# Attention step: where the turned rows and the turned context stand on TensorE, and the context copy on ScalarE

## What is computed

```python
x = x + tanh(g_xattn[0]) * attention(layernorm(x), ctx, ctx, mask, Wq, bq, Wk, bk, Wv, bv, Wo, bo)
# attention, for each sequence:
q = heads(query @ Wq + bq) / 4
k = heads(key @ Wk + bk)
v = heads(value @ Wv + bv)
scores = where(mask == 0, -1e20, q @ k.T)
out = (softmax(scores) @ v) @ Wo + bo
```

## Time and profile before

| | us |
|---|---|
| median of 3 runs | 705.67 |
| lowest, highest | 705.29, 708.04 |
| span of the profiled execution | 705.0 |
| TensorE busy in it | 640.0 (91%) |
| VectorE, ScalarE, GpSimd busy in it | 423.2, 303.0, 266.6 |

### The profile page before, as it was taken

How to read it: one execution, slowest core, us unless ns; L and a number is a source line. 1 busy time by engine, 2 the same in 40 slices (tenths; PEclk the granted TensorE clock), 3 DMA queues, 4 the chain that set the end, 5 groups by cost and what they waited for, 6 DMA issues and landing times.

```text
span 705.0 us, 14478 instructions
## 1 busy us (share of the span) xinstructions
PE 640.0 (91%) x5191; PEld 465.1 (66%) x5191; DVE 423.2 (60%) x1287; ACT 303.0 (43%) x632; POOL 266.6 (38%) x388
## 2 busy tenths in 40 slices
PE   7899999999999988869999999999899999992990
PEld 5465655777777755557656665657788888882880
DVE  6654756898999658863112222112668988883671
ACT  2323235787878825343221222220555555510750
POOL 4101202454554521043465445233211334355475
PEclk9999999999999999989999999999999999996996
DMA  8659853778775229881563894323613494123652
GB/s 276 204 155 212 220 105 87 126 130 125 125 127 92 94 75 160 269 264 32 101 146 39 243 291 96 71 30 46 223 61 121 151 308 164 61 91 102 205 163 80
DMA packets 101278, 99.95 MB, mean 142 GB/s; under 512 B 22182, under 2 KB 91305, under 8 KB 101204
## 3 DMA queue, kind: packets, MB, share of 16 engines
q1 hardware_dynamic: 91992, 82.57, 46.1%
q0 software_dynamic: 9216, 16.46, 10.3%
HBM read 61.20 MB, written 38.05 MB: 141 GB/s over the span
## 4 chain that ended last, share of the span: by engine, by line
PE 49%; DVE 6%; issue 2%; DMA 2%; POOL 2%; ACT 1%; POOLq 0%; SPq 0%; DVEq 0%; ACTq 0%
PE pc L1705 10%; PE pc L1682 9%; PE pc L2541 4%; PE pc L2274 4%; PE pc L2269 3%; PE pc L1065 3%; PE pc L2310 2%; PE pc L2267 2%; PE pc L1658 2%; PE pc L2251 2%; PE pc L1701 2%; POOL result L2446 1%; PE pc L2332 1%; PE pc L1670 1%; PE pc L1685 1%
## 5 line engine op out<-in xcount | busy, mean ns | idle before, releaser
L1522 POOL DMA_INDIRECT scratch_resid<-y,k_idx x32 | 54.8, 1714 | 81.8 <-DVE y L1590 80.9
L506 DVE TENSOR_REDUCE neg_max<-pb_two 128x8 f32<-128x1024 f32 x64 | 78.1, 1220 | 12.2 <-PE pb_two L836 9.2
L671 ACT ACTIVATE probs<-pb_two,b_key_cols 128x1024 f32<-128x1024 f32 x64 | 76.9, 1202 | 16.0 <-PE pb_two L860 16.0
L1705 PE MATMUL pc<-w_dn,mid 128*128 128x256 f32 x320 | 73.3, 384 | 0.0
L1633 ACT ACTIVATE mid<-pc,b_up 128x512 f32<-128x512 f32 x35 | 24.1, 687 | 109.7 <-PE pc L1682 109.7
L1705 PEld LDWEIGHTS pc<-w_dn,mid 128*128 128x128 f32 x320 | 59.5, 190 | 12.7 <-issue 5.3
L1682 PE MATMUL pc<-gT,w_up 128*128 128x512 f32 x140 | 61.2, 592 | 0.0
L1590 DVE TENSOR_SCALAR y<-pc,gate 128x256 f32<-128x256 f32 x32 | 15.4, 484 | 64.6 <-PE pc L1705 46.8
L1513 POOL DMA_INDIRECT rows<-scratch_rows,k_idx x32 | 32.0, 999 | 53.6 <-DVE k_idx L1366 37.9
L1682 PEld LDWEIGHTS pc<-gT,w_up 128*128 128x128 f32 x140 | 26.6, 190 | 30.5 <-issue 30.1
L1572 DVE COPY gT<-pc 128x512 f32<-128x512 f32 x7 | 4.8, 692 | 61.0 <-PE pc L1670 61.0
(11 more groups left out here) (381 smaller groups left out, 1417.5 us busy)
## 6 DMA issues: line engine op xcount, KB each, us to landing
qs<-scratch_qparts SPq DMA_DIRECT2D x48, 128.0 KB, 4.2
ks<-scratch_kparts SPq DMA_DIRECT2D x48, 128.0 KB
w_dn<-in_W_down SPq DMA_DIRECT2D x8, 640.0 KB
scratch_slots<-s_zero SPq DMA_DIRECT2D x1, 4160.0 KB, 18.8
cT<-in_ctxT SPq DMA_DIRECT2D x8, 512.0 KB, 6.5
s_x<-in_x SPq DMA_DIRECT2D x8, 512.0 KB, 6.9
scratch_rows<-s_x SPq DMA_DIRECT2D x16, 256.0 KB, 4.2
scratch_resid<-s_x SPq DMA_DIRECT2D x8, 512.0 KB, 7.1
```

The source lines that it names most:

```text
L506: V.tensor_reduce(neg_max[:].rearrange("p (b u j) -> p u b j", b=2, u=2)[:, u], ps_both[0][:].rearrange("p (b j k) -> p b j k", b=2, j=4), ...
L671: A.activation(probs[t % 2 * 2 + u][:], ps_both[1][:].rearrange("p (h q) -> p h q", h=HEADS // 2), ACT.Exp, bias=key_cols[:, 1, t:t + 1], ...
L1522: pool.indirect_dma_start(out=T["resid"], out_offset=bass.IndirectOffsetOnAxis(ap=S["idx"][:, e, c:c + 1], axis=0), in_=y[e % 2][:, c, :], ...
L1705: ins = nc.tensor.matmul(here(c), mid[e % 2][m][:, c * P:(c + 1) * P], w_dn[e % 2][:, m, :], start=False, stop=(m == MT - 2))
```

## The change

On TensorE `turn_rows` and `turn_context` leave the end of step s and stand in step s+1 behind `scores(s+4,0)`, ahead of `max_T`. On ScalarE `rows_out` comes one step later and directly behind the first exponentials, and `context_out` comes behind the second exponentials. `rows_out(t)` gets one more wait, for `max_T(t+5)`, and `max_T(t)` now waits for one copy of rows fewer, since both share bank 6. No instruction that computes is added or removed.

```diff
             def rows_out(t):
                 act.wait_ge(aT_ps, t + 1)
+                act.wait_ge(nmT_ps, min(t + 6, TILES))
...
             for s in range(1, END):
                 if is_tile(s):
                     exponentials(s, 0)
+                if is_tile(s - 3):
+                    rows_out(s - 3)
                 if is_tile(s + 2):
                     max_out(s + 2)
+                if is_tile(s):
+                    exponentials(s, 1)
                 if is_tile(s - 1):
                     context_out(s - 1)
-                if is_tile(s):
-                    exponentials(s, 1)
-                if is_tile(s - 2):
-                    rows_out(s - 2)
...
             def max_T(t):
                 pe.wait_ge(nm_s, t + 1)
-                if t >= 5:
-                    pe.wait_ge(aT_s, t - 4)
+                if t >= 6:
+                    pe.wait_ge(aT_s, t - 5)
...
                 if is_tile(s + AHEAD):
                     scores(s + AHEAD, 0)
+                if is_tile(s - 3):
+                    turn_rows(s - 3)
+                if is_tile(s - 2):
+                    turn_context(s - 2)
                 if is_tile(s + 2):
                     max_T(s + 2)
...
-                if is_tile(s - 2):
-                    turn_rows(s - 2)
-                if is_tile(s - 1):
-                    turn_context(s - 1)
```

## The result

| | before | changed |
|---|---|---|
| median of 11 runs each, us | 706.23 | 710.91 |
| ratio of changed to before, 95% interval | | 1.0052 (1.0032 to 1.0073) |
| second comparison (6 and 10 runs): median, us | 706.07 | 713.51 |
| ratio, 95% interval | | 1.0094 (1.0059 to 1.0129) |
| span of the profiled execution, us | 705.0 | 709.4 |

The change is slower, by 0.5% in the first comparison and 0.9% in the second; the intervals overlap between 0.6 and 0.7%. The medians lie 4.7 us (0.66%) and 7.4 us (1.05%) apart. A time lies 1.7 to 2.3 us over the span of its own execution (711.17 and 709.4 for the profiled one of the changed kernel). The 0.7 us between span and median before was therefore not what lies around the span: it set two different executions side by side, and by these differences the profiled one took about 707 us (an estimate), more than the median of 705.67.

What follows compares the result with a forecast made beforehand. TensorE, nearly without breaks, was taken to bound the loop, VectorE close behind. Steady steps +3.8 and filling +0.4 gave +4.2 us on a span of 705.0: 709.2, median 709.9; own range 708 to 711.5, overall range 702.5 to 713.

Steps and rivals of the forecast that it cites:

- rival C: Moved maxima come late, so six waits grow: 2.4 us more, up to 4 with a larger `output` break, 712 to 714; chance 0.14.
- filling: Pipeline start: `turn_context(0)` leaves a wait in step 1 for step 2, +0.4 us, between bounds of 0 and 1.0.
- 25 steps: Steady attention loop: each step 0.15 us longer, +3.8 us in all, some 109 us long instead of 105.2.
- draining: Last steps, without scores: longer first half traded for shorter second, same work, end of chain unchanged, 0.
- The wait for ScalarE: TensorE ahead of `shifted(s,1)`: real wait 0.11 us of 0.31 idle, in 24 steps, 2.6 us to win at most.
- The first half: TensorE's first half of a steady step, with the six turns moved in: 2.46 us after, against 1.70.
- The second half: TensorE's second half of a steady step: about 1.71 us against 2.32, closed by ScalarE (1.70) and VectorE (1.73) loops.
- The step: One steady step of the attention loop: 4.17 us against 4.02, so +0.15.
- the reason given for it: Steady step: three changes from float32 to bf16 instead of two, and two new loops, traded for one 0.11 us wait.
- The moved maxima: Maxima in SBUF 0.4 us later, about 2.2 behind the step's start; longer steps give 0.45 back, net 0.
- A: TensorE's breaks are waits, VectorE becomes the bound: 4.0 us faster, 701.7, down to 698; chance 0.14.
- B: The trade comes out even: step 4.02 to 4.08 us, 0 to +1.5, so 705 to 707.5; chance 0.27.

Runs made afterwards that it cites:

- add_bf16_full: Kernel before plus one bf16 transpose with 128x128 weights between `output` and the turned rows; second half of the step 2.38 us against 2.32.
- add_f32: Kernel before plus one float32 transpose with 128x128 weights between `output` and the turned rows; second half of the step 2.43 us against 2.32.
- context_only: Kernel before with only `turn_context` moved, behind `max_T` and ahead of the contexts, ScalarE order kept; 714.89 us against 706.88, ratio 1.0096.
- add_bf16: Kernel before plus one bf16 turn with 128x32 weights between `output` and the turned rows; second half of the step 2.63 us against 2.32.
- add_short: Kernel before plus one float32 transpose with 49x128 weights between `output` and the turned rows; second half of the step 2.66 us against 2.32.
- copy_late_alone: Kernel before with only `context_out` put behind the second exponentials, TensorE's order kept; one time of 718.2 us.
- copy_early: Changed kernel with `context_out` put back ahead of the second exponentials; 715.38 us, ratio to the kernel before 1.0112.
- drain_copy: Changed kernel with `context_out` of tile 30 put ahead of the last exponentials, in step 31 alone; one time of 709.62 us.

## Why the prediction was right, and where it was not

*The size.* Forecast +4.2 us or 0.6% and a median of 708 to 711.5. The first comparison gave 710.91, inside; the second 713.51, outside, among the numbers of rival C. The sum is right in part by luck, as its terms show (means of two traces of the changed kernel less means of three of the kernel before):

| | forecast | traces |
|---|---|---|
| up to `shifted(0,0)` | 0 | +1.6, with the same code |
| filling, to `shifted(4,0)` | +0.4 | +1.3 (-0.5 and +3.0) |
| 25 steps | +3.8 | +1.0 |
| draining, to the last `output` | 0 | +1.5 |
| all that follows | 0 | -0.4 |
| span | +4.2 | +4.9 |

The 25 steps should have taken some 109 us and took 107.8 and 106.4. The term of the steps was too large by what the stalls gave back, and terms put at nothing or little made up for it. With so few traces the terms are known to 1 us at best, the draining excepted.

*The wait for ScalarE.* Read as 0.11 and not 0.31 per step. Confirmed: with the cover in place the loads still idle for 0.20 ahead of `shifted(s,1)`. Who had taken the 7.9 us of the waits view as the prize would have expected three times too much.

*The first half.* Forecast 2.46, measured 2.42. The six turns took 0.81 from start to `max_T` (0.80 forecast). The term that was off is `max_T`: 0.08 was carried over from a place where it had been waited for; in the stream it is 0.01.

*The second half.* Forecast 1.71, measured 1.76. The break behind `output` was 0.09 where TensorE came late (0.10 forecast, 0.27 feared; the sum for the lower bound, 1.92 - 1.84, is 0.08 and not 0.09). The loop with ScalarE is what binds, but the step from the end of the exponentials to `shifted` is 0.11 there and not 0.06.

*The step.* +0.15 forecast, +0.165 measured. It is made up of 0.06 by which the turns take longer in their new place (0.81 for 0.75), 0.09 for the break behind `output`, and 0.12 to 0.13 for the new wait in the second half, less the old wait of 0.11 in the first. The two waits all but cancel; the breaks are what was lost.

*What failed is the reason given for it.* "The step had two changes from float32 to bf16 and has three" is true as a count and false as a cause. The runs showed that a change of type with full weights costs nothing, and that a change of the weights' rows or columns does. The prices were right because they were taken from rows in which both changed together. The row that told the two apart was quoted in the prediction (`max_T` cost 0.01 ahead of float32 contexts) and not read as such.

*Draining.* Forecast 0, measured +1.5. "The work is the same" overlooked three things: in steps without scores the second half is bound by ScalarE while the first still grew (steps of 3.96 and 3.93 for 3.77 and 3.78), the float32 turns now meet the float32 contexts with a break of 0.17, and the late copy makes `turn_context(30)` wait, which alone is 0.70.

*Filling.* Forecast +0.4. Not confirmed as a fixed price: 18.9 and 22.4 us in the two traces against 19.0 to 19.6 before, and the spread goes with the granted clock. At a clock of 1.00 the new order costs nothing (18.9 against 19.0). What the forecast lacked is that executions at the lower level are more frequent with it, seven of 17 against none of 21.

*The moved maxima.* In SBUF 0.4 later, as forecast: in step 14 at 178.02, 2.23 behind the step's start (2.2 forecast). That the longer steps give this back holds and more: stalls of single steps were 1.8 and 3.2 us, before 4.7 to 7.2. That is why 25 x 0.165 = 4.1 us of longer steps appear as 1.0 us between the mean stretches (107.1 against 106.1) of these few traces. The other kernels go the same way: with steps of 4.08 and 4.13 (`add_bf16_full`, `add_f32`) the stalls were 5.7 and 2.6, with 4.29 to 4.36 (`context_only`, `add_bf16`, `add_short`) 0.3 to 0.8. With the still longer steps of `copy_late_alone` (4.47) the 25 steps took 111.9, just 25 x 4.475: no stall was left.

*Rivals.* A (breaks are waits, VectorE binds) is out: the added transposes were paid for in full. B (even) is out for the step. C (late maxima) is not seen: within the 25 steps the weight loads waited 4.5 and 3.2 us for moved maxima, before 2.5, 4.5 and 3.1, so no clear growth, and that the second median of 713.51 lies in C's range is owed to other stretches.

The Trainium skill (TensorE: Matmul & The Clock Gate, Step-by-step: what each phase is for) has the next tile's weights load while the present one runs, if the row groups do not conflict or the load goes to the background buffer. The trace agrees for neighbours of one shape (0.05 between the bf16 transpose and the next) and not across the changes of tile priced above, where 0.17 to 0.34 us of idle loads show. Which of the two conditions fails there no run shows.

## What to carry to other kernels

Read the price of a wait as what is left when the releaser was early, not as the idle time that the waits view sums. Before work is moved to fill a gap on TensorE, count how often the shape of the weights changes per round: cutting one block of equal shape in two cost 0.15 us per step here, and the gap was worth 0.11. A loop with stalls in single steps gives part of a longer step back, so multiply an undisturbed step by the number of steps only as an upper bound. And compare a forecast with its result term by term: a right sum can hide wrong terms. Where two engines answer each other twice per round, filling the half with slack makes the other half the loop's bound; a copy that was moved to suit one half decides what the drain waits for.

## What was not expected of the hardware

A change of the weights' tile between 128x128 and 49 rows or 32 columns costs 0.1 to 0.2 us of TensorE's time each way, for rows as for columns: 49 rows between blocks of 128 cost 0.34 with both ways and the instruction itself, 32 columns in bf16 0.31, full bf16 0.06. A change from 51 to 49 rows shows no break, and a change of type alone costs nothing measurable.

The granted clock while the pipeline fills was 1.00, 0.91 or 0.77 over some 20 us in executions of the same or nearly the same code (0.83 in `add_short`, 0.92 in `copy_late_alone`), and the stretch took 18.8 to 19.1, 19.5 to 20.1, or 22.4 to 22.6 us with it; 0.77 was seen in the second trace of the changed kernel (22.4), in `context_only` and in `copy_early`, 1.00 in the first and in `drain_copy`. TensorE idles there between bursts for VectorE and for the moved maxima. From 121 to 124 us it was busy for 1.3 us in the first trace of the changed kernel and for 1.6 in the second; behind that the clock stayed at 1.00 in the first and was 0.50, the lower of its two levels (1.2 of 2.4 GHz), from 124 to 134 us in the second. That is most of its steps 2 and 3; the stretch shown holds the last 5 of these 10 us:

```profile
129.00:136.00 7.00, 5.98 (x77) 4.66 (x79) 4.29 (x6) 4.40 (x7) 2.47 (x5) 0.64 0.95 116
```

Taking `turn_context(0)` out of step 1 seems to make the lower level more likely. 0.77 was seen in three of the five traces of orders that do so and in none of the nine of orders that keep it there. The timed executions say the same: of those orders (changed, `context_only`, `copy_early`) 15 of 27 had a mean clock below 0.970, of the kernel before none of 21. No run moved this one call alone, so the cause is not shown.
